# A gated cross-attention and LoRA block on one core: product 1 in an order by tile and block, row transposes by DMA, column sums on TensorE

## What is computed

```python
def fake_quant(x, s, z):                       # 0..255
    return (clip(round(x / s + z), 0, 255) - z) * s
x = x + tanh(g_xattn) * matmul(fake_quant(layernorm(x), s1, z1),      # product 1
                               fake_quant(ctx, s2, z2))
h = layernorm(x)
base = h @ base_W.T                                                   # product 2
w = top-2-of-8 weights of softmax(h @ router_W.T)
inc = einsum(einsum(h, lora_A) * w, lora_B)
x = x + tanh(g_ffn) * (base + 2 * inc)
```

## Time and profile before

| | us |
|---|---|
| runs | 1165.37, 1162.96, 1163.9; median 1163.9 |
| span of the profiled execution | 1164.5 (no other time of it is listed) |
| PE busy | 1085.9 (93%) |
| DVE, ACT, POOL busy | 594.8, 297.2, 189.4 |
| first matmul of product 1 | 34.67 |
| first transpose of the second part on PE | 306.20 |

### The profile page before, as it was taken

How to read it: one execution, slowest core, us unless ns; L and a number is a source line. 1 busy time by engine, 2 the same in 40 slices (tenths; PEclk the granted TensorE clock), 3 DMA queues, 4 the chain that set the end, 5 groups by cost and what they waited for, 6 DMA issues and landing times.

```text
span 1164.5 us, 13520 instructions
## 1 busy us (share of the span) xinstructions
PE 1085.9 (93%) x5130; PEld 816.5 (70%) x5152; DVE 594.8 (51%) x876; ACT 297.2 (26%) x291; POOL 189.4 (16%) x123
## 2 busy tenths in 40 slices
PE   1678987989999999998999999989999999999998
PEld 1333433334688888887888887878888789888887
DVE  7999698976763543343237224334533343222231
ACT  6642344310241212231112113111211321111210
POOL 3766678662300000000000000000000000000000
PEclk9999998999999999999999999999999999999999
DMA  9885997647572633507242633351542614162440
GB/s 361 299 298 179 311 327 224 236 147 256 190 262 67 200 116 105 194 23 291 73 153 70 211 99 118 132 212 55 181 144 73 199 40 142 54 203 84 148 145 37
DMA packets 111051, 193.88 MB, mean 166 GB/s; under 512 B 30608, under 2 KB 32656, under 8 KB 106896
## 3 DMA queue, kind: packets, MB, share of 16 engines
q1 hardware_dynamic: 68368, 153.18, 38.1%
q10 hardware_dynamic: 42624, 39.85, 11.0%
HBM read 153.16 MB, written 33.55 MB: 160 GB/s over the span
## 4 chain that ended last, share of the span: by engine, by line
PE 71%; DVE 10%; issue 6%; POOL 6%; DMA 4%; ACT 1%; SPq 1%; ACTq 0%; DVEq 0%; POOLq 0%
PE acc L818 17%; PE acc L820 17%; PE acc L819 17%; PE acc L795 3%; POOL ctx_quant L380 3%; PE acc_even L818 3%; PE acc_even L819 3%; PE acc_even L820 3%; DMA w_stage<-in_wt 2%; DVE bn_chunks L540 2%; DVE ctx_tree_sums L591 2%; PE aT_psum L855 1%; PE aT_psum L856 1%; POOL x_group_odd L394 1%; PE aT_psum L833 1%
## 5 line engine op out<-in xcount | busy, mean ns | idle before, releaser
L818 PE MATMUL acc<-w_hi,hT_hi 128*128 128x512 f32 x896 | 353.8, 395 | 0.0
L820 PE MATMUL acc<-w_hi,hT_lo 128*128 128x512 f32 x896 | 350.3, 391 | 0.0
L819 PE MATMUL acc<-w_lo,hT_hi 128*128 128x512 f32 x896 | 349.9, 390 | 0.0
L667 DVE TENSOR_TENSOR w_lo<-w_stage,w_hi 128x1024 fp32r<-128x1024 f32 x128 | 156.6, 1224 | 320.7 <-ACT w_hi L476 318.6
L476 ACT ACTIVATE w_hi<-w_stage 128x1024 fp32r<-128x1024 f32 x128 | 135.6, 1059 | 460.3 <-PE acc L820 314.2
L820 PEld LDWEIGHTS acc<-w_hi,hT_lo 128*128 128x128 f32 x896 | 168.8, 188 | 35.9
L819 PEld LDWEIGHTS acc<-w_lo,hT_hi 128*128 128x128 f32 x896 | 169.0, 189 | 34.2
L818 PEld LDWEIGHTS acc<-w_hi,hT_hi 128*128 128x128 f32 x896 | 168.8, 188 | 33.9
L795 PE MATMUL acc<-ctx_quant,aT_even 128*128 128x512 bf16 x501 | 121.2, 401 | 10.4 <-DVE x_group_even L611 7.9
L795 PE MATMUL acc<-ctx_quant,aT_odd 128*128 128x512 bf16 x501 | 113.7, 383 | 5.0 <-DVE x_group_odd L611 4.4
L795 PEld LDWEIGHTS acc<-ctx_quant,aT_even 128*128 128x128 bf16 x512 | 52.0, 103 | 77.5 <-issue 21.8
(11 more groups left out here) (129 smaller groups left out, 1011.8 us busy)
## 6 DMA issues: line engine op xcount, KB each, us to landing
w_stage<-in_wt SPq DMA_DIRECT2D x128, 512.0 KB, 5.8
ctx_stage<-in_ctx SPq DMA_DIRECT2D x32, 1024.0 KB, 6.5
x_group_even<-x_scratch SPq DMA_DIRECT2D x16, 1024.0 KB, 10.4
residual<-x_scratch SPq DMA_DIRECT2D x64, 256.0 KB, 4.0
out<-residual ACTq DMA_DIRECT2D x64, 256.0 KB, 2.8
x_group_even<-in_x SPq DMA_DIRECT2D x8, 1024.0 KB, 9.0
x_group_odd<-in_x SPq DMA_DIRECT2D x8, 1024.0 KB, 8.1
x_scratch<-x_group_even ACTq DMA_DIRECT2D x8, 1024.0 KB, 4.9
```

The costliest lines, as they stand in the source:

```text
L667: dve.tensor_tensor(wl[s][:, :], wst[s][:, :], wh[s][:, :].bitcast(F32), ALU.subtract)\
L818: pe.matmul(out_, lh, rh, start=first, stop=False)
L819: pe.matmul(out_, lh, rl, start=False, stop=False)
L820: return pe.matmul(out_, ll, rh, start=False, stop=final)
```

## The change

Product 1 is written anew as lists, one for each kind of step. What it does:

- The 64 units go in an order of their own (`UNIT_TILE`, `UNIT_BLOCK`), tile and block mixed; unit p uses accumulator p mod 4. A column sum is taken once for each of the 8 blocks, where 16 were taken, and its term is kept in one of four buffers.
- `ctx_sums` only adds the two halves of the block (one addition on DVE, 8 slices out), and `col_sums` is 8 matmuls with ones for each block.
- All 16 tiles are transposed by DMA (`PE_TILES = 0`), from two buffers `anat` in turn.
- Tiles 0, 3, 6, 9, 12 and 13 are widened on ACT (`WIDEN_ACT`), the other ten on DVE.
- SP loads in the order of `LOAD_ORDER`; each other step has a table of slots of its own.

```diff
+LOAD_ORDER = 'xxccxcccxcccxccccxcxcccxcccxxcxccxccccccxcxcxcxc'
+UNIT_TILE = [0, 1, 2, 2, 0, 1, 3, 0, 2, 4, 3, 1, 3, 3, 2, 1, 0, 4, 5, 7, 5, 6, 4, 5, 7, 6, 6, 4, 5, 7, 6, 7, 9,
+    9, 8, 8, 11, 8, 10, 10, 10, 9, 11, 13, 11, 10, 14, 14, 11, 15, 8, 9, 15, 14, 12, 14, 15, 12, 13, 12, 13, 15,
+    12, 13]
+UNIT_BLOCK = [0, 0, 0, 1, 1, 1, 0, 2, 2, 0, 2, 2, 1, 3, 3, 3, 3, 1, 1, 0, 0, 0, 3, 2, 1, 1, 2, 2, 3, 3, 3, 2, 4,
+    5, 4, 6, 6, 5, 6, 4, 5, 6, 5, 5, 7, 7, 7, 4, 4, 5, 7, 7, 4, 5, 5, 6, 7, 6, 6, 4, 4, 6, 7, 7]
+WIDEN_ACT = [0, 3, 6, 9, 12, 13]
+PE_TILES = 0
...
+            def x_widen(t):
+                act.wait_ge(xu8_ready, t + 1)
...
+                act.activation(anat[t % 2][:, :], xu8[t % 2][:, :], ACT.Identity, bias=-MID,
+                               accum_out=asum[:, t:t + 1]).then_inc(a_by_act, 1)
...
             def ctx_sums(c):
-
                 dve.wait_ge(c_conv, CP * (c + 1))
                 if c >= 1:
-                    dve.wait_ge(block_ready, c)
+                    dve.wait_ge(col_ready, c)
+                src = ctxq[:, c % NB, :, :]
+                dve.tensor_tensor(pair[:, :, :], src[:, 0:K // 2, :], src[:, K // 2:K, :], ALU.add)\
+                    .then_inc(block_ready, 1)
...
-                pe.matmul(colp[:, :], ones[:, :], csum[:, n, :], start=True, stop=True)\
-                    .then_inc(col_ready, 1)
+            def col_sums(c):
+                pe.wait_ge(block_ready, c + 1)
+                if c >= 1:
+                    pe.wait_ge(colb_ready, c)
+                for k in range(K // 2):
+                    ins = pe.matmul(colp[:, :], ones[:, :], pair[:, k, :], start=(k == 0), stop=(k == K // 2 - 1))
+                ins.then_inc(col_ready, 1)
```

More of the change, by code:

```diff
@@ L78, with last_of_block, last_of_tile @@
+SLOTS = max(STORE_SLOT + COLADD_SLOT) + 120
+LAST_STORE = STORE_SLOT.index(max(STORE_SLOT))
+STEP = 10
+UNITS = list(zip(UNIT_TILE, UNIT_BLOCK))
+PLACE = {unit: p for p, unit in enumerate(UNITS)}
+def last_of_block(c):
+    return max(p for p, (t, b) in enumerate(UNITS) if b == c)
+def last_of_tile(t):
+    return max(p for p, (a, c) in enumerate(UNITS) if a == t)
 W_AT = {6: 0, 8: 1, 10: 2, 12: 3}
@@ L122, in build @@
         cu8 = [at(f"ctx_u8_{s}", CST + 24 * KIB + 2 * KIB * s, [P, PK, NW], U8) for s in range(2)]
[L123 to L127, removed]
+        anat = [at(f"a_rows{s}", SMALL + 4 * KIB * s, [P, D], BF16) for s in range(2)]
+        xu8 = [at(f"x_u8_{s}", SMALL + 8 * KIB + 2 * KIB * s, [P, D], U8) for s in range(2)]
+        pair = at("ctx_pair_sums", SMALL + 12 * KIB, [P, K // 2, NW], F16)
+        colb = [at(f"col_term{s}", SMALL + 20 * KIB + 2 * KIB * s, [P, NW], F32) for s in range(NB)]
         wst = [at(f"w_stage{s}", AT0 + 4 * KIB * s, [P, WK * NW], F32) for s in range(RING)]
@@ L250, in build, with wait_widened, wait_aT @@
         out_stored = [sem(f"out_stored{m}") for m in range(M)]
+        def wait_widened(eng, t):
+            if t in WIDEN_ACT:
+                eng.wait_ge(a_by_act, sum(w <= t for w in WIDEN_ACT))
+            else:
+                eng.wait_ge(a_by_dve, sum(w <= t and w not in WIDEN_ACT for w in range(TILES)))
+        def wait_aT(eng, t):
+            if t < PE_TILES:
+                eng.wait_ge(aT_ready, t + 1)
+            else:
+                eng.wait_ge(aT_moved[t % 2], 16 * sum(w % 2 == t % 2 for w in range(PE_TILES, t + 1)))
         def h_psum(g, k):
@@ L312, in _ @@
             sp.dma_start(sc[:, :], scal).then_inc(s_const, 16)
[L313 to L325, removed]
+            for i, kind in enumerate(LOAD_ORDER):
+                if kind == "x":
+                    load_x(LOAD_ORDER[:i].count("x"))
+                else:
+                    load_ctx(LOAD_ORDER[:i].count("c"))
+            sp.wait_ge(x1_stored[0], 16 * NB * 2)
+            load_group(0)
+            sp.wait_ge(pe_unit, max(last_of_tile(t) for t in range(2 * M, 3 * M)) + 1)
+            for r in range(RING):
+                load_lead(r, r)
             for X in range(RING):
@@ L449, in _ @@
             for s in range(SLOTS):
[L450 to L460, removed]
+                if s in STORE_AT and STORE_AT[s] != LAST_STORE:
+                    store_x1(STORE_AT[s])
+                if s in STD_AT:
+                    std(STD_AT[s])
+                if s in CU8_AT:
+                    ctx_to_u8(CU8_AT[s])
+                if s in COPY_AT:
+                    aT_copy(COPY_AT[s])
+                if s in MOVE_AT and MOVE_AT[s] >= PE_TILES:
+                    aT_move(MOVE_AT[s])
+                if s in QUANT_AT:
+                    x_to_u8(QUANT_AT[s])
+                if s in WIDEN_AT and WIDEN_AT[s] in WIDEN_ACT:
+                    x_widen(WIDEN_AT[s])
+                if s == B0 + STEP * M:
                     act.wait_ge(var2_ready, 1)
                     act.activation(sd[:, :], ve[:, :], ACT.Sqrt).then_inc(std2_ready, 1)
-                if s == B0 + M + 2:
+                if s == B0 + STEP * (M + 2):
                     for r in range(RING):
```

242 lines of the change are left out of this document (126 added, 116 removed), and 9 rows, old and new, of tables (COLADD_SLOT, EVAC_SLOT, UNIT_SLOT).

## The result

The changed kernel takes 1169.3 us (median of 15 runs, 1168.3 to 1173.8), the kernel before 1165.3 beside it: a ratio of 1.004, interval 1.0028 to 1.0051. It is **slower by 0.4%**, where 1148 was forecast, 1.4% faster than the 1163.9 known then. Its profiled execution has a span of 1166.9 us.

The account below looks back on a forecast made before the run. PE, busy 93%, was taken as the bound, with only the 306.2 us to product 1's end open to change: 31.7 + 234.2 + 2 + 3 + 4 + 5 + 10 = 289.9, 16.3 less, so 1148 us, range 1130 to 1163.

Parts of the forecast that it names:

- the start: Before product 1's first unit on PE: it would begin at 31.7 us, against 34.67 before.
- the first blocks: Early units of product 1: pieces come late for unit 7, costing PE 3 us.
- E: The moment product 1 ends on PE: 306.2 us in the kernel before, 289.9 forecast.
- PE's work, 234.2: PE in product 1: 220.8 us of units plus 13.4 of column-sum matmuls, transposes gone.
- the rest behind E, 858.3: The 858.3 us after product 1, in which PE doesn't pause and which the change leaves alone.
- The clock cost: Slower PE units after long pauses in product 1: three pauses at 1.7, 5 us.
- The first column sum: Behind PE's first unit: PE, free at 35.1, waits for the pair sum until 36.9, 2 us.
- The last block: Group 3's loads wait for group 1's stores, so unit 44 comes late: 4 us, from 0 to 15.
- The stall at the end: Before E, unit 60 waits for unit 56's `evac` behind DVE's statistics: 8.6 us, about 10 with a slower unit.
- the rival with 1134 to 1138: End of product 1: no stall, since the load is back early or DVE is faster; 10 us go; chance 0.25.
- the moves land late: At the start, beside saturated loads, moves land in up to 10.4 us: 7 us lost, 1155; chance 0.13.
- ACT's queue blocks: Six moves (tiles 8 to 13) hold ACT's queue 5.07 us each ahead of the last pieces: 19.3 us, 1167; chance 0.12.

Follow-up runs that it names:

- e1: The changed kernel with the transposes of tiles 0 to 3 given back to TensorE and a copy by ACT: 1169.1 us, 1.002 to the kernel before.
- e2: The changed kernel with tiles 0 to 7 transposed by TensorE: 1158.5 us, 0.9935 to the kernel before.
- e4: The changed kernel with the full tree of column sums on DVE again and one ones-matmul per block: 1178.4 us, 1.0103 to the kernel before.
- e7: The changed kernel with all row widenings on DVE, none on ACT: 1177.9 us, 1.0115 to the kernel before.
- e8: The changed kernel with all 16 tiles transposed by TensorE and copied by ACT: 1155.5 us, 0.9924 to the kernel before.
- e5: The changed kernel with tiles 0 to 7 transposed by TensorE and STEP 22 instead of 10: 1154.7 us, 0.9912 to the kernel before.
- e3: The changed kernel with STEP 30 instead of 10, spreading group 0's statistics, normalising and router split: 1166.9 us, 1.0006 to the kernel before.
- e9: The changed kernel with all 16 tiles transposed by TensorE and STEP 22 instead of 10: 1154.2 us, 0.9896 to the kernel before.
- e11: The kernel before with the first four tiles' transposes by DMA as well, from one row buffer: 1181.7 us, 1.0136 to the kernel before.
- e6: The changed kernel with SP holding load 19 and all behind it until tile 4's move has landed: 1168.2 us, 1.0033 to the kernel before.

## Why the prediction was wrong

**The step that failed is the price of the moves**, at three terms of the sum: the start (31.7), the first blocks (3) and the cover that groups 0 and 1 were given. The moves were priced by the earlier trace rows, 1.33 to 5.07 us in ACT's queue and 4.3 to land. Those rows are of tiles 4 to 15 in the old order; the new moves stand beside the first loads, at 339 GB/s from 9 to 28 us, and that of tile 4 beside 386 GB/s. The longest now are 9.13 in the queue and 20.3 to land, both nearly twice the 5.07 and 10.4 that I had taken from the rows as their ends.

By terms: the start is 37.1 for 31.7 (5.4). Pauses of PE after that come to 27.1 for the 17.6 forecast (2 + 3 + 4 + 8.6): 13.2 at the start and the first blocks for 5, 6.9 in the middle for 4, 6.9 at the end for 8.6. With 234.2 of work that leaves 10.6 for slower units for about 6.4. 5.4 + 9.5 + 4.2 = 19.1, which is the miss in E. The first two go with the moves: with those of tiles 0 to 3 on TensorE the first unit starts at 32.3 (e1), and with those of tiles 0 to 7 the 13.2 are 2.4 (e2).

Point by point:
- PE's work, 234.2, and the rest behind E, 858.3: right (857.9). The clock cost was right by its kind, and too small since there were more pauses.
- DVE's waits go with the tree and the widenings: right, and e4 and e7 show it.
- An ACT widening at 2.1: right, 1.91 and 0.18 for its accumulator.
- The first column sum, 2 us behind the first unit: 0.45. The pair sum was as late as the unit, at 43.1 for 36.9, and the unit took 5.61 for 3.45. (33.8 and 2.84 make 36.6 and not 36.9, a slip of 0.3.)
- Group 0's last unit at 106 and group 1's at 160: wrong, 120.6 and 174.1. This is the start and tile 4, passed on.
- The last block: I expected a pause of 4 at unit 44. It was 0.2, by luck: the loads began at 195.0 for 163, the last piece was widened at 229.34, and PE was itself late enough to come there at 229.2 (204.8 in the forecast). The pause is at the column sum of block 5 and unit 35. The move issued at 149.66 held ACT's queue for 7.52, with a piece behind it; with all transposes on TensorE (e8) the pause isn't there, with tiles 8 to 15 moved (e2, e5) it is. That the 7.52 is its cause and not the moves' share of the DMA engines wasn't separated.
- The stall at the end, 8.6 and a slow unit: right in place and mechanism, 6.9 and a slow unit, as e3 measured. That the whole time falls by its full size once it is gone (the rival with 1134 to 1138) is refuted by e3 and e9, for this way of removing it.
- The rivals: "the moves land late" and "ACT's queue blocks" are both what happened. The first I bounded at 10.4 us of landing and so at 1155; the second I placed at tiles 8 to 13 alone, at 5.07 each. Its result, E = 309, is the measured one, but not by its working: those six moves stood 20.5 us in the queue, 9.4 over the median, and the larger loss lay at tiles 1 and 4.
- The rule of the Trainium skill ("VectorE: DVE Perf Modes", The three transpose paths), 20.9 us for a move as an estimate, I set aside because the median landing was 4.3. The median after is 5.0, so as a general price it doesn't hold here. For tile 4 (20.3; 22.4 in e1) and the first move of e11 (17.5), beside full loads, it was close. The ruling was right for a move with few loads beside it (4.3 for those at 107.03 and 163.48, with 9 and 15% of the engines' time for loads) and was applied to one beside full loads (92%).

## What to carry to other kernels

Price a transfer by rows of the stretch into which it is put, not by the median of where it stood: in a stretch where the DMA engines are full, a 0.5 MB transpose stood up to 9 us in its engine's queue and took up to 22 us to land, and work queued behind the issue pays for the first, work that needs the rows for the second. A transpose on TensorE of 1.06 us that has its own place in PE's order was the cheaper one here, even on the busiest engine. And before you take a stall out at the end of a stage, look at what the next stage waits for: of 8 to 10 us removed ahead of E, 1 to 4 reached the time, and what made room there put the next stage's weights back by 2 to 4.

## What the runs showed of the hardware

- The time to land of the same 0.5 MB transpose went from 4.2 to 22.4 us; with the loads beside it held back (e6), the one of tile 4 went from 20.3 to 5.2.
- Issuing a DMA transpose can hold ACT's queue with all its data ready: 9.13 us at 23.70 and 7.52 at 149.66, against 1.33 at the least. At both times the DMA engines were full (share 1.08 from 28 to 32 us, 1.01 from 130 to 174). But full engines alone don't do it: the three moves that took longest to land (20.3, 22.4 in e1, 17.5 in e11) were issued in 1.44, 1.60 and 1.44, with a share of 0.99 to 1.06 in the 3 us ahead; and in the kernel before one stood 4.86 at 181.53 with a share of 0.00 ahead of it. What sets the hold stays open.
- Per byte the transpose costs the engines more than a load: from the q rows of e6, 47.2% of 5.2 us for 0.52 MB are 4.7 us of all 16 engines a MB, and 51.2% for the loads' 0.99 MB are 2.7. (Their packets are some 250 bytes and 2.0 KB.)
